# A two-layer perceiver kernel on one core: the 257th key by transposed weights, and loads in the order of first use

## The reference

```
q = norm(x) Wq + bq ; k = ctx Wk + bk ; v = ctx Wv + bv      (257 keys)
p = softmax(q k^T / sqrt(8) + mask)                          (mask in layer 0 only)
x = x + (p v) Wo + bo
```

## Time and profile before

| what | value |
|---|---|
| median of 3 runs | 1186.34 us (1184.51 to 1186.34) |
| the profiled execution, device time | 1192.6 us |
| its span (first to last instruction) | 1191.0 us |
| PE busy | 1128.8 us, 95% |
| DVE, ACT, POOL busy | 816.2 (69%), 721.2 (61%), 532.9 us (45%) |
| mean granted TensorE clock | 0.974 of full |

### The profile page before, as it was taken

How to read it: one execution, slowest core, us unless ns; L and a number is a source line. 1 busy time by engine, 2 the same in 40 slices (tenths; PEclk the granted TensorE clock), 3 DMA queues, 4 the chain that set the end, 5 groups by cost and what they waited for, 6 DMA issues and landing times.

```text
span 1191.0 us, 35107 instructions
## 1 busy us (share of the span) xinstructions
PE 1128.8 (95%) x13192; PEld 942.5 (79%) x13192; DVE 816.2 (69%) x2833; ACT 721.2 (61%) x2241; POOL 532.9 (45%) x712
## 2 busy tenths in 40 slices
PE   5998999998999999999999999999999999999887
PEld 3677878777788887888888788888888788887676
DVE  2757877678685876868677676867867577676653
ACT  2972665864667757566765656767565665836442
POOL 4696243456254554634445353454634344252220
PEclk9998999999999999999999999999999899999897
DMA  9520000010000000100000010000000000000000
GB/s 286 192 52 20 1 2 6 22 36 23 4 22 22 22 22 4 38 4 22 22 22 22 2 26 18 22 22 19 23 3 4 2 4 2 2 4 2 4 3 4
DMA packets 17731, 30.73 MB, mean 26 GB/s; under 512 B 2200, under 2 KB 14752, under 8 KB 16928
## 3 DMA queue, kind: packets, MB, share of 16 engines
q1 hardware_dynamic: 15264, 27.45, 7.7%
q10 hardware_dynamic: 2304, 1.05, 0.3%
HBM read 27.44 MB, written 1.05 MB: 24 GB/s over the span
## 4 chain that ended last, share of the span: by engine, by line
PE 70%; DVE 15%; POOL 6%; issue 4%; ACT 3%; DMA 1%; SPq 0%; DVEq 0%; POOLq 0%
PE bank L971 15%; PE bank L979 12%; PE bank L855 9%; PE bank L848 6%; PE bank L867 5%; PE bank L937 4%; PE bank L822 3%; PE bank L815 3%; DVE xs L1305 3%; PE bank L881 2%; PE bank L956 2%; POOL rstd L710 2%; DVE xn L1151 1%; DVE P L1295 1%; POOL vtb L790 1%
## 5 line engine op out<-in xcount | busy, mean ns | idle before, releaser
L971 PE MATMUL bank<-xnT,w 128*128 128x128 f32 x2048 | 258.2, 281 | 0.2 <-DVE P L1288 0.2
L971 PEld LDWEIGHTS bank<-xnT,w 128*128 128x128 f32 x2048 | 243.5, 195 | 9.7 <-issue 7.4
L1030 ACT COPY PT<-bank 128x512 f32<-128x512 f32 x256 | 148.8, 587 | 26.2 <-PE bank L855 24.5
L855 PE MATMUL bank<-cst,P 128*128 128x128 f32 x1024 | 156.0, 282 | 5.0 <-ACT P L1022 4.6
L1022 ACT ACTIVATE P<-bank,nmax 128x257 f32<-128x257 f32 x256 | 121.1, 488 | 40.8 <-DVE nmax L1166 39.7
L855 PEld LDWEIGHTS bank<-cst,P 128*128 128x128 f32 x1024 | 116.3, 143 | 31.3 <-issue 22.6
L1162 DVE CUSTOM_DVE_ANT_0 P<-bank,maskb,mscale 128x257 f32<-128x257 f32 x256 | 113.8, 480 | 39.0 <-PE bank L848 38.4
L979 PE MATMUL bank<-w2b,P 128*128 128x128 f32 x1024 | 135.0, 285 | 0.6 <-ACT P L1022 0.6
L1019 ACT ACTIVATE P<-P,nmax 128x257 f32<-128x257 f32 x256 | 130.9, 513 | 6.4 <-DVE nmax L1162 6.2
L979 PEld LDWEIGHTS bank<-w2b,P 128*128 128x128 f32 x1024 | 126.4, 200 | 4.2 <-issue 1.5
L1166 DVE TENSOR_REDUCE nmax<-bank 128x1 f32<-128x257 f32 x256 | 95.4, 414 | 38.3 <-PE bank L848 38.1
(11 more groups left out here) (135 smaller groups left out, 2263.1 us busy)
## 6 DMA issues: line engine op xcount, KB each, us to landing
ctxT<-ctx_in SPq DMA_DIRECT2D x16, 522.0 KB, 3.6
maskb<-mask_in SPq DMA_DIRECT2D x64, 128.5 KB, 2.9
w<-w_in SPq DMA_DIRECT2D x2, 2048.0 KB, 18.7
w2b<-w2b_in SPq DMA_DIRECT2D x1, 2048.0 KB, 26.4
wsq<-wsq_in SPq DMA_DIRECT2D x1, 1224.0 KB
xin<-x_in SPq DMA_DIRECT2D x16, 64.0 KB, 2.6
w2a<-w2a_in SPq DMA_DIRECT2D x1, 1024.0 KB, 17.4
out<-xs ACTq DMA_DIRECT2D x16, 64.0 KB, 1.5
```

The lines of the kernel that those rows point to most:

```text
L855: ins = nc.tensor.transpose(ps[:, k * 128:k * 128 + 128], P[s][:, 2 * m + k // 2, (k % 2) * 128:(k % 2) * 128 + 128], ident)
L971: ins = nc.tensor.matmul(ps[:, k * 128:k * 128 + 128], wt[:, m, k * 128:k * 128 + 128], xnT[s][:, :], start=True, stop=True)
L1030: nc.scalar.copy(PT[:, place, m % 2 * 512:m % 2 * 512 + 512], ps[:, :]).then_inc(pt_done[s], 1)
```

## The change

Two edits, and with them a new order.

1. **Tail.** The tail's value is now made with features on the partitions, like its key (PE "kvtail": two products with 128x4 output; DVE copies both). Once the weights of a group and layer are done, POOL copies column 257 of `P` into `tails`, each value repeated 32 times (128x512). PE transposes that in 4 pieces into a bank of its own; ACT copies it into `On` in 4 pieces, each scaled by the tail's value of that sequence; DVE adds the pv bank to `On`. "rT" is no longer copied by ACT: "norm" multiplies `On` by the bank of "rT" directly. "tailT", `vtb`, `vtl` and the constant `tail_block` (512 columns of the constants) go away.
2. **Start.** SP loads the bias columns and the three weights used first (384 of the columns of `wsq`) ahead of everything, the context and `x` of stream 0, then the constants, and the rest of the weights, the rows of biases, the router and `b2` only after the loads of stream 2's context and `x`. Engines wait for the first two loads alone and for the others where they need them. `bo` is a step of the planner.
3. **Order.** The costs and needs of the steps are changed accordingly, all priorities in `BONUS` are new numbers, and each of the 16 groups gets a priority of its own (`WHEN`). So the order on all engines is another one.

The diff, cut to its core:

```diff
 def step_parts(kind, l, m):
-        "vproj": ((PE, 4 * MM), (VACT, .47)), "kvtail": ((PE, .65), (DVE, .42), (POOL, 1.25)),
+        "bo": ((PE, 4 * MM), (DVE, .65)), "vproj": ((PE, 4 * MM), (VACT, .47)), "kvtail": ((PE, .3), (DVE, .3)),
...
-        "tailT": ((PE, TR), (VACT, .2)), "tailV": ((PE, 4 * MM),),
-        "sel": ((DVE, .17), (POOL, 1.02)), "rT": ((PE, 4 * TR + .05), (VACT, .47)),
+        "tailV": ((POOL, 1.02), (PE, 4 * TR + .05), (VACT, .85), (DVE, .65)),
+        "sel": ((DVE, .17), (POOL, 1.02)), "rT": ((PE, 4 * TR + .05),),
...
-        add("tailT", l, 0, ("soft", l, U - 1, VACT))
-        add("tailV", l, 0, ("tailT", l, 0, VACT), ("pv", l, GB - 1, PE), ("kvtail", l, 0, POOL))
+        add("tailV", l, 0, ("soft", l, U - 1, VACT), act=[("kvtail", l, 0, DVE), ("bo", 0, 0, DVE)], dve=[("pv", l, GB - 1, PE)])
...
-    prio = [behind[t] - (i * STREAMS + s) * LAG + BONUS.get((t[0], t[1], t[3]), 0.0) for s, t, i in names]
+    prio = [behind[t] - (i * STREAMS + s) * LAG + BONUS.get((t[0], t[1], t[3]), 0.0) + WHEN[i * STREAMS + s] for s, t, i in names]
...
         def _(sp):
-            for dst, src in ((cst[:, :], const_d), (bcol[:, :], bcol_d), (rows_in, brow_d[:, 0:512]),
-                             (router[:, :], brow_d[:, 512:520]), (wsq[:, :], wsq_d),
-                             (b2[:, :], b2_d)):
-                sp.dma_start(dst, src).then_inc(constants_in, 16)
+            for dst, src in ((bcol[:, :], bcol_d), (wsq[:, 0:WFIRST], wsq_d[:, 0:WFIRST])):
+                sp.dma_start(dst, src).then_inc(first_in, 16)
...
             for s in range(STREAMS):
                 load_ctx(0, s)
                 load_x(0, s)
+                if s == 0:
+                    sp.dma_start(cst[:, :], const_d).then_inc(constants_in, 16)
+                elif s == STREAMS - 1:
+                    for dst, src in ((wsq[:, WFIRST:WSQ], wsq_d[:, WFIRST:WSQ]), (rows_in, brow_d[:, 0:512]),
+                                     (router[:, :], brow_d[:, 512:520]), (b2[:, :], b2_d)):
+                        sp.dma_start(dst, src).then_inc(others_in, 16)
                 load_mask(0, s)
...
         def _(pool):
-            pool.wait_ge(constants_in, 16 * SETUP_LOADS)
+            pool.wait_ge(first_in, 16 * FIRST_LOADS)
+            pool.wait_ge(constants_in, 16)
...
-            pool.wait_ge(bo_done, 1)
...
+                    if (i, l, m) == (0, 0, 0):
+                        pool.wait_ge(bo_done, 1)
                     src = xin[s] if (l, m) == (0, 0) else xs[s]
...
-                elif kind == "kvtail":
-                    pool.wait_ge(kvtail_done[s], at(i, l, 2, 2))
-                    nc.gpsimd.tensor_tensor(vtb[s][:, :].rearrange("p (b f) -> p b f", b=GB),
-                                            vtl[s][:, :].unsqueeze(1).broadcast_to((U, GB, 128)),
-                                            c("tail_block", U).rearrange("p (b f) -> p b f", b=GB),
-                                            ALU.mult).then_inc(vtail_done[s], 1)
+                elif kind == "tailV":
+                    pool.wait_ge(exp_done[s], at(i, l, U, U))
+                    nc.gpsimd.tensor_copy(tails[s][:, :, :], P[s][:, :, KM].unsqueeze(2).broadcast_to((128, U, 32))
+                                          ).then_inc(tails_done[s], 1)
...
         def _(pe):
-            pe.wait_ge(constants_in, 16 * SETUP_LOADS)
-            pe.wait_ge(jscaled_done, 1)
...
+            pe.wait_ge(first_in, 16 * FIRST_LOADS)
...
                     nc.tensor.matmul(ps[:, 0:4], w(f"k{l}"), ctxT[s][:, t:t + GB], start=True, stop=True)
-                    nc.tensor.matmul(ps[0:U, 16:16 + 128], ctxT[s][:, t + GB:t + GB + U], w(f"v{l}"),
-                                     start=True, stop=True).then_inc(full, 1)
+                    nc.tensor.matmul(ps[:, 4:8], w(f"v{l}"), ctxT[s][:, t:t + GB], start=True,
+                                     stop=True).then_inc(full, 1)
...
-                elif kind == "tailT":
-                    pe.wait_ge(exp_done[s], at(i, l, U, U))
-                    nc.tensor.transpose(ps[0:U, 0:128], P[s][:, :, KM], ident).then_inc(full, 1)
                 elif kind == "tailV":
-                    pe.wait_ge(tail_done[s], at(i, l, 1, 1))
-                    pe.wait_ge(vtail_done[s], at(i, l, 1, 1))
-                    ps = bank[bank_of[("pv", s, l, 0), i, 0]]
+                    pe.wait_ge(tails_done[s], at(i, l, 1, 1))
                     for b in range(GB):
-                        ins = nc.tensor.matmul(ps[:, 128 * b:128 * b + 128],
-                                               vtb[s][:, 128 * b:128 * b + 128], tT[s][:, :], start=False,
-                                               stop=(b == GB - 1), skip_group_check=True)
-                    ins.then_inc(attn_done[s], 1)
+                        ins = nc.tensor.transpose(ps[:, 128 * b:128 * b + 128],
+                                                  tails[s][:, NGR * b:NGR * b + NGR, :], ident)
+                    ins.then_inc(full, 1)
...
         def _(act):
...
-                elif kind == "tailT":
-                    wait_full(act, i, step)
-                    nc.scalar.copy(tT[s][:, :], ps[0:U, 0:128]).then_inc(tail_done[s], 1)
-                elif kind == "rT":
-                    wait_full(act, i, step)
-                    nc.scalar.copy(On[s][:, :, :, :].rearrange("p j b s -> p b j s"),
-                                   ps[:, :].rearrange("p (b j s) -> p b j s", b=GB, j=J)).then_inc(rT_done[s], 1)
+                elif kind == "tailV":
+                    wait_full(act, i, step)
+                    if (i, l) == (0, 0):
+                        act.wait_ge(bo_done, 1)
+                    act.wait_ge(kvtail_done[s], at(i, l, 2, 2))
+                    for b in range(GB):
+                        ins = nc.scalar.activation(
+                            On[s][:, :, b, :], ps[:, 128 * b:128 * b + 128].rearrange("p (j s) -> p j s", j=J),
+                            ACT.Copy, scale=vt[s][:, l, b:b + 1])
+                    ins.then_inc(tail_done[s], 1)
...
         def _(dve):
...
-                    wait(dve, vtail_done[s], 2 * i + l)
-                    nc.vector.tensor_copy(vtl[s][:, :], ps[0:U, 16:144]).then_inc(kvtail_done[s], 1)
+                    nc.vector.tensor_copy(vt[s][:, l, :], ps[:, 4:8]).then_inc(kvtail_done[s], 1)
...
+                elif kind == "tailV":
+                    dve.wait_ge(tail_done[s], at(i, l, 1, 1))
+                    dve.wait_ge(pv_done[s], at(i, l, GB, GB))
+                    sums_on = On[s][:, :, :, :].rearrange("p j b s -> p b j s")
+                    ps = bank[bank_of[("pv", s, l, 0), i, 0]]
+                    nc.vector.tensor_tensor(sums_on, ps[:, :].rearrange("p (b j s) -> p b j s", b=GB, j=J), sums_on,
+                                            ALU.add).then_inc(on_done[s], 1)
```

More of the change, by code:

```diff
@@ L73, in step_parts @@
     return {
-        "mask": ((POOL, 3.8), (DVE, 1.3)), "kproj": ((PE, 4 * MM), (VACT, .58)),
-        "vproj": ((PE, 4 * MM), (VACT, .47)), "kvtail": ((PE, .65), (DVE, .42), (POOL, 1.25)),
+        "bo": ((PE, 4 * MM), (DVE, .65)), "mask": ((POOL, 3.8), (DVE, 1.3)), "kproj": ((PE, 4 * MM), (VACT, .58)),
+        "vproj": ((PE, 4 * MM), (VACT, .47)), "kvtail": ((PE, .3), (DVE, .3)),
         "ln": ((DVE, .53), (POOL, .78)), "xpb": ((POOL, .45),),
@@ L99 @@
 BANKS = {"scores": NGR, "sscore": NGR, "pv": 1, "spv": 1}
-FILLS = ("kproj", "vproj", "kvtail", "lnT", "qproj", "scores", "ptrans", "tailT", "rT", "oproj", "qk", "vself",
+FILLS = ("bo", "kproj", "vproj", "kvtail", "lnT", "qproj", "scores", "ptrans", "tailV", "rT", "oproj", "qk", "vself",
          "lines", "linesT", "jlines", "sscore", "sptrans", "route", "up", "down", "wT", "wb2")
 ARRIVES = {("mask", 0): 6.0, ("kproj", 0): 6.0, ("ln", 0): 5.0, ("xpb", 0): 5.0, ("oproj", 0): 3.0}
-FIRST = {("mask", POOL): 17.0, ("kproj", PE): 13.0, ("ln", DVE): 14.0, ("xpb", POOL): 14.0, ("up", PE): 45.0}
-LATER = 6.0
+FIRST = {("kproj", PE): (4.8, 9.7, 13.6), ("ln", DVE): (5.2, 10.0, 13.9), ("xpb", POOL): (5.2, 10.0, 13.9),
+         ("mask", POOL): (7.9, 11.8, 19.5), ("bo", PE): (20.5,), ("up", PE): (30.0, 30.0, 30.0)}
+BEGIN = 4.0
 def banks_of(kind, l, m):
@@ L161, in group_tasks @@
         for m in range(2):
[L162 removed]
+            add("xpb", l, m, *([("oproj", l, 0, DVE)] if m else [x_from] if l else [("bo", 0, 0, DVE)]))
             if m:
@@ L176, in group_tasks @@
                 add("spv", l, 0, ("sptrans", l, 0, VACT), ("vself", l, 0, VACT))
-            add("norm", l, m, *([("spv", l, 0, PE)] if m else [("rT", l, 0, VACT), ("tailV", l, 0, PE)]))
+            add("norm", l, m, *([("spv", l, 0, PE)] if m else [("rT", l, 0, PE), ("tailV", l, 0, DVE)]))
             add("oproj", l, m, ("norm", l, m, POOL), dve=[("xpb", l, m, POOL)])
@@ L197, in group_tasks @@
         ("vproj", 0, 0, PE): [("pv", 1, GB - 1, PE)],
-        ("kvtail", 0, 0, PE): [("tailV", 1, 0, PE), ("scores", 1, GB - 1, PE), ("kvtail", 1, 0, POOL)],
```

(29 more changed lines are left out.)

157 lines of the change are left out of this document (80 added, 77 removed).

## The result

The changed kernel takes **1177.08 us** (median of its five runs, four of them between 1175.88 and 1178.53) against 1186.34 for the kernel before: a ratio of 0.9919, interval 0.9898 to 0.9941, so 9.3 us or 0.8% faster. The other run, at a granted clock of 0.741, took 1359.76 us and is left out of the ratio. The forecast was 1152, its range 1136 to 1170: the sign was right, and three quarters of the 34.4 us did not arrive.

The account below looks back on a forecast made before the run. The prediction took PE, busy for 95% of the span, to bound the kernel. Tail 28.3 us plus start 6.1 us, with the order at zero, made 34.4 us off: 1186.3 to 1152 us, range 1136 to 1170.

Parts of the forecast that it names:

- Part 1, the tail on PE: PE's "tailV", "tailT" and "kvtail": 0.885 us saved per group and layer, 28.3 us in all, 1.77 of each turn.
- the rival with half pace: Tail transposes on PE take 0.22 us each, so the tail gives only 16.6 us: 1164 us; chance 0.02.
- Part 1, elsewhere: ACT gains 18 to 28 us of work, DVE 22 us, POOL about even; all covered by PE, costing nothing.
- The rival in which PE stands behind POOL: At "tailV", a POOL copy 3.7 us late each turn holds PE: 31 us lost, less 6.1, 1211 us; chance 0.07.
- Part 2, the start: Setup loads and first "kproj": it starts at 6.0 instead of 13.02 us; net gain 6.1 us, between 0 and 8.
- Part 3, the order: New order on all engines: taken as zero; bounds 17 us gained at the end or the 100-200 us stretch's loss.
- covered by PE's 98% in the turn: In the turn, added ACT, DVE and POOL work costs nothing; each has 19 us or more to spare in 69.8.
- the other two fill PE meanwhile: A group's chain grows by up to 2.3 us per layer, costed at nothing with three groups in flight.
- The work leaves PE but not the time: In the turn, another wait such as a held bank returns half of 28.3 us as idle: 1166 us; chance 0.18.
- The end gets shorter too: Last three groups end side by side, 14 of 17.4 us idle at the end go: 1138 us; chance 0.20.
- the signs named beforehand: Wrong if: turns 69 us or more with `tails` or bank waits, "kproj" after 9, transposes 0.22, or last stretch changed.

Follow-up runs that it names:

- the two new orders: Kernel before and changed kernel, each with its order searched anew in the same way on costs read from traces: 1161.35 us and 1133.78 us.
- the old order: Changed kernel with new tail and start, each step's priority taken from the plan of the kernel before: 1184.69 us, ratio 0.9978.
- C's queue: Theory C: the second round's first mask queues behind expert weights. Changed kernel with second-layer expert loads issued behind nine reloads: 1169.90 us, ratio 0.9842.
- theory B: Claim that the new tail's longer chain and held banks make PE stand in any order; changed kernel with only its order searched anew: 1133.78 us.
- its new order: Changed kernel with only its order searched anew, on costs read from traces and the first new mask planned late: 1133.78 us, ratio 0.9542.

## Why the prediction was wrong

**Part 1, the tail on PE: right.** "tailV" 0.44 us in the rows above for the 0.515 taken, "kvtail" 0.37 for 0.42, no row transposes: the sum of 28.3 us, 1.77 of each turn, stands beside 2.05 us in the turn, 29.9 between the two profiles and 29.6 between the two new orders. The transposes keep 0.11 us each at a granted clock of 1.00, so the rival with half pace is out; the rule of the Trainium skill, page "TensorE: Matmul & The Clock Gate", section "Part 4: PE-mode transpose", that the full clock does not engage for them is not what this row shows.

**Part 1, elsewhere: right where it did not matter.** POOL's copy takes 0.62 us, not 1.04; ACT's pieces and DVE's pass take what was priced. The rival in which PE stands behind POOL did not come at "tailV": 0.0 us before L894. What it describes, a mask pass on POOL that holds PE, happened once at another step: POOL's pass from 42.99 us stood in front of the "norm", and PE waited 3.7 us for that at 48 us.

**Part 2, the start: right at its place.** First "kproj" at 5.82 us for 6.0. (The 1.07 MB up to the constants are 1.08 by the sizes issued, which changes nothing.) "The third mask and the expert loads move behind about the same bytes as before" came true: they were issued at 11.1 and 12.9 us, before at 11.3 and 13.4. But the working stops there, and the loads after them were not looked at: with work starting earlier, the first mask of the second round was issued at 32 us instead of 41 and landed only 9.68 us after its last issue, behind the experts. That was worth 7.2 us.

**Part 3, the order: "I take zero" is the step that failed.** What it says of gains held. Little was to be won in the middle (28.6 us of idle time before, 22.8 and 22.3 in the two orders planned on read durations), and of the 17 us at the end 10.0 came. What failed is its bound for a loss: it took the one stretch from 100 to 200 us, 7.4 us, and the time from 30 to 1100 us lost 29.7. An order that is laid down for one set of durations is a part of the price: the kernel before gave back some 5 of 14.4 us when only work was removed, the old order gave back all but 3.3 us of the whole change (with C's queue in it), the changed kernel's own order gave back 25 of 34.4, and orders planned on read durations let 27.6 through. With it fails "covered by PE's 98% in the turn", and that the longer chain costs nothing because "the other two fill PE meanwhile". Both were read off the old order. They hold in an order that has the other groups' work at the right place, and are no property of the work.

**The rivals.** "The work leaves PE but not the time" had the right outcome and the wrong cause: it blamed banks and hand-overs of the new tail, which theory B tested and lost. It also took half of the tail for its size. In the changed kernel the time from 30 to 1100 us took back 29.7 us, as much as the tail saved, and the shorter end and the start are what is left. "The end gets shorter too" came for the end itself, 10.0 us of the 14 it priced. Of the signs named beforehand two showed: turns of 69.0 us, though without the waits on `tails` named with them, and a last stretch that has clearly changed.

## What to carry to other kernels

Where every engine follows an order fixed at build time, price an edit together with the re-planning of the order: work taken off the bounding engine comes back in part as idle time unless the order is planned again, here with durations read from a trace. Compare two variants only with orders that were searched in the same way; here the same change measured 3.3, 9.3 or 27.6 us depending on the orders it was measured in. And when loads are moved to the front, follow the queue on to the first reload, not only to the last setup load.

## What was not expected of the hardware

A stand of PE is paid twice. In five profiles the same 13032 matmuls kept PE busy for 1107.0 us at a mean granted clock of 0.974, 1100.7 at 0.981, 1098.9 at 0.983, 1089.1 at 0.989 and 1085.7 at 0.992: a spread of 21 us with no change of work. The product of the two is 1077 to 1080 us in all five, so most of the spread goes with the clock. In stages of 5 us the fall comes right after idle time. In the changed kernel:

```profile
40.00:45.00 5.00, 4.34 (x48) 1.00 0.17 39
45.00:50.00 5.00, 1.75 (x22) 0.95 0.33 105
50.00:55.00 5.00, 5.00 (x27) 0.71 0.43 109
55.00:60.00 5.00, 4.87 (x78) 1.00 0.00 0
...
80.00:85.00 5.00, 3.24 (x64) 1.00 0.03 7
85.00:90.00 5.00, 1.49 (x6) 0.71 0.34 103
90.00:95.00 5.00, 5.00 (x25) 0.61 0.00 0
95.00:100.00 5.00, 5.00 (x46) 1.00 0.01 3
```

PE is idle for 3.3 of 5 us, and in the next 5 us it is busy throughout at a mean clock of 0.71; after 3.5 idle us it is 0.61. The Trainium skill, page "TensorE: Matmul & The Clock Gate", section "Why this matters for your kernels", warns that the clock falls back after idle gaps between bursts of matmuls, and these rows agree with that much. Of the 42 us between the spans of the changed kernel and of the same kernel in its new order, 9.8 are busy time and 32.4 are idle time. The rise of the mean clock from 0.983 to 0.989 accounts for some 6.7 of the 9.8 (an estimate: 1098.9 x 0.006 / 0.989).
